# High one-hots of the edge count: a difference on GpSimd, square and floor on ScalarE, in place of a comparison on VectorE

## The reference

```
x = x + L0_gnn(layernorm(x), edge_weight, src, dst)   # a product of 100,000 plane rotations
x = x + L0_ffn(...)    # one expert of eight per node
x = x + L1_gnn(...)    # graph attention over the edges, 8 heads
x = x + L1_ffn(...)    # one linear layer
x = x + L2_gnn(...)    # sum over neighbours, linear, batch norm
x = x + L2_ffn(...)    # two experts of eight
x = x + L3_gnn(...)    # one GCN and two attention layers, with self loops
x = x + L3_ffn(...)    # two experts of eight
```

## Time and profile before

| | us |
|---|---|
| median of 3 runs | 8527.33 |
| lowest and highest | 8518.01, 8529.29 |
| the profiled execution | 8529.27 |
| its span | 8527.5 |
| phase of `edge_tables` in it, first to last instruction | 1131.8 to 1320.0 |
| counting loop in it, first one-hot to the copy of the sum | 1159.7 to 1313.9 |

### The profile page before, as it was taken

The page is one execution under the profiler, slowest core; times in us unless marked ns, Lnnn a source line. Parts: engine busy times, 40 slices in busy tenths (PEclk is TensorE's granted clock), DMA queues, the critical chain, the costliest instruction groups (busy, mean ns, idle before and its releaser), DMA issues. The chain is left out here.

```text
span 8527.5 us, 99058 instructions
## 1 busy us (share of the span) xinstructions
PE 5287.1 (62%) x21044; PEld 3982.8 (47%) x21045; DVE 3825.3 (45%) x9108; ACT 3279.2 (38%) x7862; POOL 4613.8 (54%) x4841
## 2 busy tenths in 40 slices
PE   3269935777744555568954443556777577777596
PEld 2156634554433444445643333335555455556464
DVE  5643385777770000054540000256666566666354
ACT  0042303444434333334533333234443344445353
POOL 5021105777736777632217777677776677773421
PEclk9569956777776777769965555567777777776698
DMA  2144412444423333332221111134443344442323
GB/s 59 74 158 175 161 35 79 117 116 116 116 58 112 104 104 104 91 101 68 63 81 27 26 26 26 46 105 110 110 110 95 92 111 111 111 111 73 117 63 128
DMA packets 414772, 786.94 MB, mean 92 GB/s; under 512 B 117865, under 2 KB 267467, under 8 KB 407667
## 3 DMA queue, kind: packets, MB, share of 16 engines
q0 software_dynamic: 208304, 507.09, 21.6%
q1 hardware_dynamic: 196486, 236.49, 8.8%
q10 hardware_dynamic: 9532, 39.01, 1.1%
HBM read 600.84 MB, written 187.29 MB: 92 GB/s over the span
## 5 line engine op out<-in xcount | busy, mean ns | idle before, releaser
L717 POOL DMA_INDIRECT g_rows<-table,src_idx x2352 | 2238.3, 952 | 717.6 <-issue 717.0
L992 PE MATMUL g_p_win<-g_rows,g_hot 128*128 128x264 f32 (+1 forms) x4704 | 1523.3, 482 | 44.4 <-issue 41.3
L992 PEld LDWEIGHTS g_p_win<-g_rows,g_hot 128*128 128x128 f32 x4704 | 1083.7, 242 | 310.7 <-issue 92.2
L882 ACT ACTIVATE g_hot<-iota,near 128x128 f32<-128x128 f32 x2352 | 720.6, 386 | 436.3 <-PE g_p_win L992 389.3
L717 POOL DMA_INDIRECT g2p_rows<-rows,src_idx x784 | 751.4, 958 | 239.0 <-issue 239.0
L717 POOL DMA_INDIRECT gcnp_rows<-table,src_idx x784 | 750.4, 957 | 239.3 <-issue 239.3
L798 DVE TENSOR_TENSOR g_rows<-g_rows,g_p_w 128x1792 f32<-128x1792 f32 x336 | 679.1, 2021 | 27.0 <-ACT g_rows L910 2.7
L2337 POOL DMA_INDIRECT back<-e_y,e_idx x210 | 205.8, 980 | 706.4 <-DVE e_idx L2428 542.0
L949 PE MATMUL g_p_turn<-slide,g_a 128*8 128x128 f32 (+1 forms) x168 | 60.9, 362 | 730.8 <-DVE g_a L757 730.8
L901 ACT ACTIVATE g_resets_f<-fwd_reset 128x112 f32 (+3 forms) x168 | 54.9, 327 | 1177.9 <-DVE g_b L769 1066.0
L805 DVE TENSOR_TENSOR agg<-agg,g2p_p_out 128x256 f32 x112 | 42.1, 418 | 960.7 <-PE g2p_p_out L954 960.7
(11 more groups left out here) (737 smaller groups left out, 11016.7 us busy)
## 6 DMA issues: line engine op xcount, KB each, us to landing
g_rows<-table,src_idx POOLq DMA_INDIRECT x2352
expert_rows<-e_zero SPq DMA_DIRECT2D x28, 1332.5 KB
c_row<-back SPq DMA_DIRECT2D x35, 896.0 KB, 7.5
e_xin<-expert_rows SPq DMA_DIRECT2D x210, 130.0 KB, 2.1
expert_rows<-e_zero SPq DMA_DIRECT2D x13, 970.0 KB
back<-agg ACTq DMA_DIRECT2D x7, 1792.0 KB, 34.2
g_inj<-inject SPq DMA_DIRECT2D x56, 224.0 KB
g2p_rows<-rows,src_idx POOLq DMA_INDIRECT x784
```

The costliest lines, as they stand in the source:

```text
L717: gp.indirect_dma_start(rows[:, s, j, 0:width + H], None, table, bass.IndirectOffsetOnAxis(g.src_idx[:, at:at + 1], 0)).then_inc(got[s], 16)
L882: last = nc.scalar.activation(hot[:, j, :], g.iota[:, :], ACT.Square, scale=-1.0, bias=g.near[:, bass.ds(c * J + j, 1)])
L992: last = nc.tensor.matmul(p_win[:, 0:W], hot[:, j, :], rows[:, s, j, :], start=(j == 0), stop=(j == J - 1))
```

## The change

The high one-hots are no longer made by VectorE. Three steps on two other engines take their place, chunk by chunk, each with two buffers:

1. GpSimd subtracts: `apart = iota - hi`, a tensor_tensor of 686 bf16 elements a partition. It begins when `hot_free` has reached 2 and waits for chunk c until the squares of chunk c - 2 are made (`squared`, which starts at 2).
2. ScalarE squares: `apart2 = apart * apart`.
3. ScalarE floors: `hot_hi = relu(1 - apart2)`, after a wait for its own square and for `hot_free`.

VectorE keeps the low one-hots alone. TensorE waits for `hot` (now one a chunk) and then for `hot_high`. Where one engine waits for two semaphores in a row, a no-operation stands between them.

```diff
--- before.py
+++ after.py
@@ -153,6 +153,7 @@
         more, more_to, more_from = ph.sb("more", [1, NC]), ph.sb("more_to", [1, NC]), ph.sb("more_from", [1, NC])
         hot_lo = ph.sb("hot_lo", [P, 2, J, P], BF16)
         hot_hi = ph.sb("hot_hi", [P, 2, J, NT], BF16)
+        apart, apart2 = ph.sb("apart", [P, 2, J, NT], BF16), ph.sb("apart2", [P, 2, J, NT], BF16)
         zero_b = ph.sb("zero_b", [P, P], BF16)
         tri = ph.sb("tri", [NT, NT])
         deg = ph.sb("deg", [NT, P])
@@ -167,7 +168,8 @@
         p_first = ph.ps("p_first", [P, NC])
         blank, d_in, s_in, no_src, rs_done = (ph.sem(n) for n in ("blank", "d_in", "s_in", "no_src", "rs_done"))
         ops, rs_t, rs_ready = ph.sem("ops"), ph.sem("rs_t"), ph.sem("rs_ready")
-        hot, hot_free, deg_done, deg_ready, off_done, t_done = (ph.sem(n) for n in ("hot", "hot_free", "deg_done", "deg_ready", "off_done", "t_done"))
+        hot, hot_high, hot_free, deg_done, deg_ready, off_done, t_done = (ph.sem(n) for n in ("hot", "hot_high", "hot_free", "deg_done", "deg_ready", "off_done", "t_done"))
+        parted, squared = ph.sem("parted"), ph.sem("squared")
         stored, tri_ready, firsts, first_done = ph.sem("stored"), ph.sem("tri_ready"), ph.sem("firsts"), ph.sem("first_done")
         dst, src = g.dst_dram, g.src_dram
         full = NC - 1
@@ -200,6 +202,15 @@
 
                 nc.gpsimd.affine_select(out=tri[:, :], in_=tri[:, :], compare_op=ALU.is_ge, fill=1.0,
                                         base=0, pattern=[[-1, NT]], channel_multiplier=1).then_inc(tri_ready, 1)
+
+                gp.wait_ge(hot_free, 2)
+
+                def high_hots(c, s):
+                    gp.wait_ge(squared, c + 1)
+                    gp.nop(nofuse=True)
+                    nc.gpsimd.tensor_tensor(apart[:, s, :, :], iota_b[:, 0:NT].unsqueeze(1).to_broadcast([P, J, NT]),
+                                            hi[:, bass.ds(c, 1), :].rearrange("p a j -> p (a j)").unsqueeze(2).to_broadcast([P, J, NT]), ALU.subtract).then_inc(parted, 1)
+                by_two(gp, NC, high_hots)
 
             @block.vector
             def _(dv):
@@ -266,8 +277,6 @@
                     dv.wait_ge(hot_free, c + 1)
                     nc.vector.tensor_tensor(hot_lo[:, s, :, :], iota_b[:, :].unsqueeze(1).to_broadcast([P, J, P]),
                                             lo[:, bass.ds(c, 1), :].rearrange("p a j -> p (a j)").unsqueeze(2).to_broadcast([P, J, P]), ALU.is_equal).then_inc(hot, 1)
-                    nc.vector.tensor_tensor(hot_hi[:, s, :, :], iota_b[:, 0:NT].unsqueeze(1).to_broadcast([P, J, NT]),
-                                            hi[:, bass.ds(c, 1), :].rearrange("p a j -> p (a j)").unsqueeze(2).to_broadcast([P, J, NT]), ALU.is_equal).then_inc(hot, 1)
                 by_two(dv, NC, hots)
                 dv.wait_ge(deg_done, 1)
                 ch.do(nc.vector.tensor_copy(deg[:, :], p_deg[:, :]))
@@ -295,6 +304,20 @@
                 ch.do(nc.vector.tensor_copy(g.first_edge[:, :], p_t[:, 1, :]))
                 ch.do(nc.vector.tensor_scalar(g.no_edges[:, :], g.deg[:, :], 0.0, None, ALU.is_equal))
 
+            @block.scalar
+            def _(ac):
+                nc.scalar.sem_inc(squared, 2)
+
+                def high_hots(c, s):
+                    ac.wait_ge(parted, c + 1)
+                    nc.scalar.activation(apart2[:, s, :, :], apart[:, s, :, :], ACT.Square).then_inc(squared, 1)
+                    ac.wait_ge(squared, c + 3)
+                    ac.nop(nofuse=True)
+                    ac.wait_ge(hot_free, c + 1)
+                    ac.nop(nofuse=True)
+                    nc.scalar.activation(hot_hi[:, s, :, :], apart2[:, s, :, :], ACT.Relu, scale=-1.0, bias=g.ones[:, 0:1]).then_inc(hot_high, 1)
+                by_two(ac, NC, high_hots)
+
             @block.tensor
             def _(pe):
                 pe.wait_ge(firsts, 1)
@@ -306,7 +329,9 @@
                 nc.tensor.matmul(p_deg[:, :], zero_b[:, 0:NT], zero_b[:, :], start=True, stop=False, skip_group_check=True)
 
                 def count(c, s):
-                    pe.wait_ge(hot, 2 * (c + 1))
+                    pe.wait_ge(hot, c + 1)
+                    pe.nop(nofuse=True)
+                    pe.wait_ge(hot_high, c + 1)
                     for j in range(J):
                         last = nc.tensor.matmul(p_deg[:, :], hot_hi[:, s, j, :], hot_lo[:, s, j, :], start=False, stop=False, skip_group_check=True)
                     last.then_inc(hot_free, 1)
```

## The result

The changed kernel takes 8544.48 us (median of 17 runs, 8538.86 to 8547.34), the kernel before 8526.42 (17 runs, 8518.01 to 8532.12): 18 us more, a ratio of 1.002 with a 95% interval of 1.0013 to 1.0028, so slower by 11 to 24 us.

The account below looks back on a forecast made before the run. VectorE bounds the counting loop; with turns the period becomes 1.87 + 1.42 - 0.17 = 3.12 us, 56 of them +22.5 us, plus 1 us around it: 8552.8 us profiled, median 8551. Own range 8543 to 8563, whole range 8518 to 8586.

Parts of the forecast that it names:

- VectorE bounds the stage, and losing L269 alone would save 44 us: Counting loop: VectorE is saturated; removing the high one-hots, 0.783 us per chunk, would by itself save 44 us.
- ScalarE 1.8 to 2.2 us a chunk, no table load: Counting loop: ScalarE's square, floor and waits take 1.8 to 2.2 us a chunk, under any period above it.
- The two engines take turns, and the period is the sum: Counting loop: VectorE's low one-hot and GpSimd's difference exclude each other; turns of 1.87 and 1.25 us, period 3.12 us.
- P = 1.42 us: GpSimd's time alone for one chunk's difference: 1.42 us, between 1.34 and 1.45; break-even at 1.02 us.
- The turn saved: Counting loop: a turn that was waited for is shorter than the instruction alone, 0.14 us on VectorE, 0.17 on GpSimd.
- The first chunk: Loop start: needs a turn of each engine, a square and a floor before its matmuls; within a +1 us allowance.
- The sum: Whole loop: 56 periods of 3.12 us, 174.7 against 152.2, +22.5 us; with 1 us around it, +23.5 us.
- the 1 us reserved for the ends: Around the loop: the first chunk's start and three more semaphores to clear, +1 us for both.
- (a): Counting loop: the two engines do not exclude each other in bf16; period about 1.97, 42 us saved, 8485 us; chance 0.11.
- (b): Counting loop: exclusion, but GpSimd quick, 0.70 to 1.29 us alone; -17 to +16 us, around 8527; chance 0.15.
- (c): Counting loop: GpSimd slow in this form, 1.65 to 1.96 us alone; +36 to +54 us, 8563 to 8581; chance 0.17.
- (d): Counting loop: ScalarE's chain of waits is the bound, over 3.12 us; at 3.5, +45 us, 8572; chance 0.03.

Follow-up runs that it names:

- The first experiment: The changed kernel with the low one-hots' row read from PSUM, not SBUF: 9534.9 us, ratio 0.9947 to the kernel before on the same chip.

## Why the prediction was right, point by point

- *VectorE bounds the stage, and losing L269 alone would save 44 us.* Right: with the turns taken away the loop lost 43.
- *ScalarE 1.8 to 2.2 us a chunk, no table load.* 0.775 + 0.866 us and 0.15 between them make 1.79; fed without a gap, as at times in the kernel with the row in PSUM, it does a chunk in 1.68. The estimate was a little high, and nothing depended on it.
- *The two engines take turns, and the period is the sum.* Right, and the step that decided. Turns of 1.20 and 1.88 us were measured, 1.25 and 1.87 forecast. The first experiment shows that the second operand in SBUF is what makes the low one-hot wait.
- *P = 1.42 us.* Mis-sized by 0.08: the first difference, which did not have to wait, took 1.345. That is the 1.34 of the line through L1359's two sizes; the 0.08 that I added towards L1137, for two full operands and a register in the address, was not there. The difference has the register and not the full operands, so L1137's 730 ns probably belong to its operands; no run here separates the two. The turn saved a little less than I took (0.14 for 0.17). Together the period was 3.084 and not 3.12: 2 us of the loop. The 2.6 cycles an element of the Trainium skill, "GPSIMD Engine Reference", section "Elementwise — side-by-side cycle accounting", would have given an estimate of 1.55 to 1.66. The measurement, 1.345, decides against it for this form, with a repeated operand.
- *The first chunk.* The sum counts 56 full periods, the first difference's turn among them. It began at 1158.69, before VectorE's first one-hot, because the signal was given by VectorE's queue before L270 had run; L270 has one input in PSUM, and neither slowed the other (952 and 1345 ns). That saved most of the first turn: from the first low one-hot to the second it is 1.99 us and not 3.08, 1.1 us less.
- *The sum.* +23.5 forecast, +19.4 in the loop, +18 (11 to 24) in the medians. The 4 us are the period (56 x 0.036 = 2.0), the first turn (1.1), and the 1 us reserved for the ends, of which less than 0.1 was seen: 56 x (3.084 - 2.718) = 20.5, less 1.1, is the measured 19.4. All three go the same way, so the median came out near the lower end of the forecast's own range, 8544.5 in 8543 to 8563.
- *Rivals.* (a), no exclusion in bf16, fell with the change's own rows, and its price was about right for the kernel that has no exclusion (loop -43 against the -42 I gave). (b) and (c) were matters of P and fell with 1.345. (d) fell with the row in PSUM, where the same chain went round in 1.956.

## What to carry to other kernels

Work that moves from VectorE to GpSimd is not moved if both instructions read two operands from SBUF: the two engines' times add, and the gain is only what the second engine's version is cheaper by. Here it was dearer (1.20 us a turn for 0.78). Two engines can so hold each other up where no semaphore stands between them, and both then read as fully busy. Before such a move look for a VectorE instruction in the trace that is longer than usual while GpSimd runs; if there is one, try the kernel with one of VectorE's operands in PSUM. Of the two, only VectorE's number of inputs in SBUF was varied: a GpSimd instruction with one input tensor was not run.

## What the runs showed of the hardware that was not expected

- A constant operand in PSUM frees the other engine at hardly any price: 2002 ns for the low one-hot against 2006, and beside a running GpSimd 2018.
- Who comes first has the turn, and a waiting instruction has the next one. Turns need not alternate: with the difference made twice, VectorE had nothing in hand when the spare difference ended (1303.48), and GpSimd took the second turn in a row; VectorE's instruction came at 1304.10 and began its turn when that one ended.
- Two inputs in SBUF are not the only case. The prediction's own rows have a cast with one input that waited, and the instruction behind it, a tensor_scalar with one input tensor, waited for GpSimd's next L1359 (6582.15 to 6584.04). In the kernel before each also runs once where no L1359 is near (5457.7 us), in 0.164 and 0.172 us:

```profile
L1228 DVE CAST n_whof<-n_who x2: 164/1012/1861, 5457.7 to 6580.3; 128x8 f32<-128x8 int32 x2
6582.24 1.83 DVE L1229 TENSOR_SCALAR n_mask<-n_whof 128x8 f32<-128x8 f32 x1
```

  Such a cast may wait even for an instruction that only writes: in the run with the memset, VectorE's cast of 1 x 56 elements just before the loop (L270 there) lasted 0.78 us where it takes 0.20 in the changed kernel, and ended 0.07 us after GpSimd's first memset. That is one instance, and no run here tells which one-input instructions wait and which do not.
- With the period at 1.956 us the granted clock of TensorE, 0.50 through the whole loop before, was 0.59 and then 0.77 and 0.79 of full speed in the stretches shown, means between its two levels of 1.2 and 2.4 GHz. Before it first rose TensorE stood idle 0.27 to 0.39 us ahead of a chunk; in the kernel before it was 1.03 us. At the upper level it stood idle for 1.0 to 1.1 us, and the clock fell again: it is 0.50 from 1245 to 1250 us. Stretches of the kernel with the row in PSUM, in the columns of the earlier trace rows:

```profile
1224.00:1240.00 16.00, 9.75 (x94) 8.55 (x95) 15.95 (x14) 12.56 (x17) 13.00 (x10) 0.59 0.02 5
1240.00:1260.00 20.00, 12.64 (x144) 10.89 (x142) 19.98 (x11) 15.81 (x21) 13.82 (x11) 0.77 0.00 0
1280.00:1300.00 20.00, 12.22 (x141) 10.54 (x142) 19.98 (x12) 15.87 (x21) 14.55 (x11) 0.79 0.00 0
```

Its 14 matmuls of a chunk, early and late in the loop:

```profile
1229.49 1.66 PE L338 MATMUL edge_p_deg<-edge_hot_lo,edge_hot_hi 128*49 128x128 bf16 x14 [0.27 <-DVE edge_hot_lo L280]
1307.83 0.94 PE L338 MATMUL edge_p_deg<-edge_hot_lo,edge_hot_hi 128*49 128x128 bf16 x14 [1.01 <-DVE edge_hot_lo L280]
```

1.66 us at the lower level (granted 0.50 from 1228 to 1230 us) and 0.94 at the upper (1.00 from 1307.8 to 1308.8). It gave nothing back, since VectorE set the period.
